# Graph layer and expert layer on one core: the window sums get a full copy, and ten saves of the node rows become one behind the weights

## What is computed

```python
# part 1: graph layer
xs = x[src]
for r in range(4):
    w_r = where(edge_type == r, edge_weight, 0)
    total_msg += (xs @ W_rel[r] + b_rel[r]) * w_r[:, None]
agg = segment_sum(total_msg, dst) / max(segment_sum(edge_weight, dst), 1)
x1 = layer_norm(x + x @ W_self + b_self + agg)
out = layer_norm(x1 + gelu(x1 @ W_ffn1 + b_ffn1) @ W_ffn2 + b_ffn2)
# part 2: 16 experts, the 2 best of each node, on x + out
out = sum_e gate_e * (gelu(xt @ w1e.T + b1e) @ w2e.T + b2e)
```

## Time and profile before

| | |
|---|---|
| median of 3 runs | 654.05 us (651.04 to 654.9) |
| the profiled execution | 651.04 us, of it 649.1 us span |
| PE busy | 528.2 us (81%) |
| DVE busy | 318.7 us (49%) |
| ACT busy | 109.2 us (17%) |
| POOL busy | 228.1 us (35%) |
| chain that ended last | PE 72%, DVE 8%, POOL 7%, DMA 6%, issue 5% |

### The profile page before, as it was taken

One profiled execution on the slowest core, in us unless ns is written; L12 is line 12 of the kernel. 1 busy time (PEld: TensorE's weight loads), 2 busy tenths in 40 slices (PEclk: granted clock), 3 DMA queues, 4 the chain that ended last, 5 costly groups with the idle time before them and its releaser, 6 DMA issues.

```text
span 649.1 us, 7246 instructions
## 1 busy us (share of the span) xinstructions
PE 528.2 (81%) x2292; PEld 355.9 (55%) x2293; DVE 318.7 (49%) x845; ACT 109.2 (17%) x230; POOL 228.1 (35%) x269
## 2 busy tenths in 40 slices
PE   0799999999974999999999999539369879889400
PEld 0588888887722665756657667223046557666200
DVE  5597564321317045986976885857102222222144
ACT  0601011000011322222213212011022222222000
POOL 2750000017777677776773000004700011110173
PEclk9999999989988899999999999855569999999855
DMA  8544342228999676766674492432425477773186
GB/s 291 192 154 149 120 162 97 89 92 259 278 354 354 188 204 199 205 197 182 203 201 126 186 409 87 166 161 114 202 89 176 159 249 264 263 265 113 67 246 223
DMA packets 47682, 125.47 MB, mean 193 GB/s; under 512 B 6480, under 2 KB 7120, under 8 KB 45344
## 3 DMA queue, kind: packets, MB, share of 16 engines
q0 software_dynamic: 17344, 63.20, 31.8%
q1 hardware_dynamic: 27056, 54.95, 22.7%
q10 hardware_dynamic: 3248, 6.89, 3.4%
HBM read 85.70 MB, written 39.32 MB: 193 GB/s over the span
## 4 chain that ended last, share of the span: by engine, by line
PE 72%; DVE 8%; POOL 7%; DMA 6%; issue 5%; ACT 1%; POOLq 0%; SPq 0%; ACTq 0%; DVEq 0%
PE ps L811 11%; PE ps L822 10%; PE ps L751 7%; PE ps L752 7%; PE ps L753 7%; PE ps L944 7%; PE ps L961 6%; PE ps L777 6%; POOL greg L562 3%; DMA greg<-xslot 3%; POOL xslot L536 3%; PE ps L937 2%; PE ps L788 2%; PE ps L843 1%; PE ps L790 1%
## 5 line engine op out<-in xcount | busy, mean ns | idle before, releaser
L515 POOL DMA_INDIRECT greg<-msg,row_i x157 | 153.0, 974 | 156.4 <-DMA msg<-greg 101.6
L751 PE MATMUL ps<-w_hi,xT_hi 128*128 128x512 f32 x200 | 80.0, 400 | 1.7 <-DVE xT_lo L1038 1.7
L752 PE MATMUL ps<-w_lo,xT_hi 128*128 128x512 f32 x200 | 79.5, 398 | 0.0
L753 PE MATMUL ps<-w_hi,xT_lo 128*128 128x512 f32 x200 | 79.3, 397 | 0.0
L811 PE MATMUL ps<-freg,wreg 128*128 128x256 f32 x320 | 72.2, 385 | 0.8 <-ACT freg L610 0.8
L822 PE MATMUL ps<-wreg,freg 128*128 128x512 f32 x160 | 72.1, 598 | 0.0
L811 PEld LDWEIGHTS ps<-freg,wreg 128*128 128x128 f32 x320 | 60.6, 192 | 16.5 <-issue 7.5
L944 PE MATMUL ps<-wreg,freg 128*128 x224 | 56.6, 398 | 0.0
L961 PE MATMUL ps<-wreg,freg 128*128 x112 | 52.7, 593 | 0.9 <-ACT freg L697 0.9
L1342 DVE COPY freg<-ps 128x256 f32<-128x256 f32 x28 | 11.9, 425 | 80.2 <-PE ps L944 80.2
L777 PE MATMUL ps<-greg,sel 128*32 128x512 f32 x320 | 45.6, 629 | 6.8 <-DMA greg<-msg,row_i 6.3
(11 more groups left out here) (169 smaller groups left out, 641.8 us busy)
## 6 DMA issues: line engine op xcount, KB each, us to landing
wreg<-experts POOLq DMA_DIRECT2D x11, 1025.0 KB, 6.8
msg<-greg SPq DMA_DIRECT2D x40, 256.0 KB, 2.0
xslot<-greg SPq DMA_DIRECT2D x1, 8960.0 KB, 25.6
greg<-xslot SPq DMA_DIRECT2D x28, 256.0 KB, 3.8
yslot<-greg SPq DMA_DIRECT2D x28, 256.0 KB, 2.8
wreg<-experts SPq DMA_DIRECT2D x5, 1025.0 KB, 9.4
wreg<-w SPq DMA_DIRECT2D x8, 512.0 KB, 13.6
w_in<-w_rel ACTq DMA_DIRECT2D x3, 1024.0 KB, 6.1
```

Of the source, the lines that this page charges most:

```text
L515: nc.gpsimd.indirect_dma_start(gath[:, c % RING, :], None, msg, bass.IndirectOffsetOnAxis(ap=row_i[:, c:c + 1], axis=0)).then_inc(s_gath[c ...
L751: nc.tensor.matmul(bank(t % 5), xT_hi[:, at], w_hi[:, i, wk], start=(k == 0), stop=False)
L752: nc.tensor.matmul(bank(t % 5), xT_hi[:, at], w_lo[:, i, wk], start=False, stop=False)
L753: mm = nc.tensor.matmul(bank(t % 5), xT_lo[:, at], w_hi[:, i, wk], start=False, stop=(k == KD - 1))
```

## The change

It has two parts. The sums of each step are copied to a new buffer `q_all` in SBUF first, a second pass over the bank makes `q_hi`, and VectorE works out `q_lo` from `q_all`; the next window sums wait for ScalarE's two copies instead of VectorE. And the ten writes of `own_rows` become one write of 2560 KB, issued behind the eight loads of the weights.

```diff
@@ the buffers
+        q_all = sb("q_all", [P, D])
@@ SyncE
-            for t in range(NT):
-                sp.wait_ge(s_evac, FREE + NT * REL + t + 1)
-                sp.dma_start(own_rows[t * P:(t + 1) * P, :], work[:, t, :]).then_inc(s_own, 16)
             sp.wait_ge(s_prod, NT * (REL + 1))
             for k in range(KD):
                 sp.dma_start(w1_v[:, k, :], w1[k * P:(k + 1) * P, :]).then_inc(s_ffw, 16)
             for k in range(0, KF, 2):
                 sp.dma_start(w2_v[:, k:k + 2, :],
                              w2[k * P:(k + 2) * P, :].rearrange("(k p) n -> p k n", p=P)).then_inc(s_ffw, 16)
+            sp.wait_ge(s_evac, FREE + NT * (REL + 1))
+            sp.dma_start(own_rows.rearrange("(t p) d -> p t d", p=P), work[:, :, :]).then_inc(s_own, 16)
+
             sp.wait_ge(s_zeros, 1)
@@ ScalarE
             def sums_out(s):
                 act.wait_ge(s_q, s + 1)
+                after(act, s_qlo, s)
+                nc.scalar.copy(q_all[:, :], bank(B_Q)).then_inc(s_qc, 1)
                 after(act, s_l2, s - 1)
                 nc.scalar.copy(q_hi[:, s % 2, :], bank(B_Q)).then_inc(s_qc, 1)
@@ TensorE
             def window_sums(s):
-                after(pe, s_qlo, s)
+                after(pe, s_qc, 2 * s)
@@ VectorE
             def low_sums(s):
-                dve.wait_ge(s_qc, s + 1)
+                dve.wait_ge(s_qc, 2 * s + 2)
                 after(dve, s_l2, s - 1)
-                v.tensor_tensor(q_lo[:, s % 2, :], bank(B_Q), q_hi[:, s % 2, :], ALU.subtract).then_inc(s_qlo, 1)
+                v.tensor_tensor(q_lo[:, s % 2, :], q_all[:, :], q_hi[:, s % 2, :], ALU.subtract).then_inc(s_qlo, 1)
@@ VectorE, ahead of fast_first_norm(0)
-                    dve.wait_ge(s_own, 16 * NT)
+                    dve.wait_ge(s_own, 16)
```

## The result

The changed kernel takes 676.29 us (median of 4 runs, 674.59 to 677.49) against 654.13 us (4 runs of the kernel before): a ratio of 1.0348, 95% interval 1.0312 to 1.0384, or 22.2 us more. The forecast was 676.5. The profiled execution took 674.45 us, of it 672.5 us span.

What follows compares the result with a forecast made beforehand. Between 184 and 211 us, VectorE's, the weights' and the gathers' strands meet at TensorE, which bounds the chain (72%). Save wait 22.0, clock 0.9 and copy 0.3 make 23.2 us; between two bases, 676.5 us, range 667 to 685.

Steps and rivals of the forecast that it cites:

- The place of the loss and its price: VectorE's norm of tile 0 waits for the save, starting at 216.7 instead of 194.69 us: 22.0 us.
- The rate of the queue: SyncE's queue: weights land at about 204.4 us, then the save at 204 GB/s beside gathers, its last 0.25 MB at 368.
- the 207 GB/s that equal turns were to give: Save beside gathers: equal turns between queues would give it 207 of 414 GB/s, next to the forecast's own 204.
- The strand moves as a piece: From tile 0's norm to tile 1's transposes (194.69 to 210.78 us) no slack; all shifts together, plus 0.9 us for the clock.
- The copy: ScalarE's added copies to `q_all` delay `q_lo` in the pair loop's rounds 1 and 2: 0.3 us, bounds 0 and 1.2.
- the spot that the prediction called tight: End of VectorE's run in the pair loop: `q_lo` ready at 280.22 us, TensorE's add at 280.33, 0.1 us of slack.
- (a): Rival: the save runs almost free of the gathers, landing at 211.5 us, 16.8 late; 669 to 672 us; chance 0.08.
- single-transfer fit: Skill page's formula, 2.0 us plus bytes at 436 GB/s: 8.0 us for the save, landing at 212.4.
- (b): Rival: the second copy is uncovered in all 15 pair-loop steps, 8.9 us on top; 683 to 686 us; chance 0.06.
- (c): Rival: the save lands by 194.69 us, before tile 0's norm, so not slower; 648 to 654 us; chance 0.02.
- (d): Rival: the save overtakes the weights, TensorE's transposes wait for them, about +7 to +8 us; 659 to 662; chance 0.03.
- The base: Starting time for the sum: profiled execution 651.04 us gives 674.2, three-run median 654.05 gives 677.3; forecast set at 676.5.

Runs made afterwards that it cites:

- e5: Kernel before, no `q_all`, the save as one 2560 KB write behind the weights, issued twice, VectorE waiting for both: 680.92 us beside 654.27, ratio 1.0406.
- e6: Kernel before, no `q_all`, the save as one 2560 KB write on ScalarE's queue while SyncE issues the weights: 668.85 us, ratio 1.023.
- e7: Kernel before with only the copy to `q_all`, its ten early saves kept: 652.43 us beside 654.27, ratio 0.9984.
- e4: Kernel before, no `q_all`, the save as one 2560 KB write ahead of the weights, after all ten tiles: 699.75 us, ratio 0.9989, on a slower chip.
- e3: Kernel before, no `q_all`, the ten 256 KB writes kept as ten but moved behind the weights: 711.35 us, ratio 1.0172, on a slower chip.
- control: Kernel before with only one register operation added ahead of each of 39 expert-stage waits: 695.0 us beside 693.56, ratio 1.0064.

## Why the prediction was right

*The place of the loss and its price.* Right. The save landed 37.7 us after the first weight was issued (180.71 to 218.41); the prediction had 37.6 (179.1 to 216.7). What shifted the landing was the products' end, 1.6 us later in this execution. In five kernels whose products are the same it lies between 177.9 and 181.1 on the chips without late sums, so this belongs to the execution, not to the change. Of the 23.7 us by which the norm starts later, 22.1 are left for the change, where 22.0 was forecast.

*The rate of the queue.* Right, but for its end. The last weight landed 25.0 us after the first was issued (it went out at 184.8 and took 20.9 us, to 205.7), where the prediction had 25.3, and the save 12.7 us behind it, where it had 12.3. From 205 to 214 us the two queues moved 209 and 204 GB/s, where it had 210 and 204. The end was wrong: it took the gathers to have landed by 216 and the last 0.25 MB of the save to go alone at 368 GB/s, in 0.7 us. The queues from 214 to 219 us:

```profile
q0 software_dynamic: 400, 1.31, 66.3%
q1 hardware_dynamic: 141, 0.26, 13.5%
```

The gathers' backlog took the engines, and the save's last 0.26 MB lasted until it landed at 218.4. The two misses, 0.3 and 0.4 us, nearly cancel. The rate of a write alone was met only in e5. And the 207 GB/s that equal turns were to give took all packets as equally large: by e6 those of the save hold 2.05 KB and the gathers' 3.28, so equal turns would give the save less than half. It got 204 because the gathers asked for no more than their pitch.

*The strand moves as a piece.* Right: 17.0 us from the norm to the transposes in the changed kernel, and in e5 (224.15 to 241.17) and e6 (211.98 to 229.05) too, for 16.1 before. The 0.9 us of it are the add at the clock's lower level: `add_windows(4)` took 2.26 us from 225.85 for 1.27 before, with a granted clock of 0.50.

*The copy.* 0.3 us was forecast, with bounds of 0 and 1.2; it cost 0.5, in round 1 alone, and at the spot that the prediction called tight. Round 1, from the sums of step 9 to those of step 13, takes 43.49 us before (255.29 to 298.78), 43.98 in the changed kernel (279.22 to 323.20) and 43.99 in e7 (255.01 to 299.00), where the copy stands alone. The changed kernel there, VectorE and then TensorE, for the earlier trace rows:

```profile
303.98 0.71 DVE L1128 TENSOR_TENSOR q_lo<-q_all,q_hi 128x512 fp32r<-128x512 f32 x1
```

```profile
301.06 3.70 PE L825 MATMUL ps<-wreg,freg 128*128 128x512 f32 x8
304.79 0.47 PE L791 MATMUL ps<-q_hi,shift 128*128 128x512 f32 x1
```

`q_lo` is ready at 304.69 and the add starts 0.10 us later. Before it was ready at 280.22 and the add started at 280.33, and the prediction read 0.1 us of slack. There was more. Matmuls overlap, so the start of the add's first row says little; its second row, the one that reads `q_lo`, says what TensorE lost. Before, in round 1, then in round 2, where `q_lo` was ready 0.5 us ahead of the add:

```profile
277.13 3.70 PE L822 MATMUL ps<-wreg,freg 128*128 128x512 f32 x8
280.90 0.39 PE L790 MATMUL ps<-q_lo,shift 128*128 128x512 f32 x1
...
320.60 3.70 PE L822 MATMUL ps<-wreg,freg 128*128 128x512 f32 x8
324.37 0.40 PE L790 MATMUL ps<-q_lo,shift 128*128 128x512 f32 x1
```

In both it starts 3.77 us behind the product's start, so round 1 lost nothing before. In the changed kernel it is 4.04 us (301.06 to 305.10): 0.27 us lost. The next add loses 0.21 in the same way (3.89 for 3.68 us). Counted from the round's start, `q_lo` starts 24.76 us in, for 24.24 before: VectorE's run in the round starts later by most of one copy of 0.59 us, and of the 0.5 us about a half was covered at the first of these adds. In round 2 nothing shows. e5 and e6, which have no copy, take 43.48 us for round 1, as before.

The total of 226.8 us hides this, because the part ahead of round 1 was shorter. Its first stretch, from the sums of step 5 to those of step 6, in the changed kernel, in e7 and in e5:

```profile
236.49:248.21 11.72, 11.72 (x56) 7.66 (x55) 0.96 (x2) 4.83 (x8) 6.03 (x6) 0.85 0.38 101
```

```profile
212.11:223.98 11.87, 11.87 (x55) 7.80 (x54) 0.96 (x2) 4.84 (x8) 8.30 (x10) 0.84 0.66 185
```

```profile
242.22:253.56 11.34, 11.34 (x56) 7.65 (x55) 0.95 (x2) 4.35 (x7) 5.93 (x7) 0.88 0.42 108
```

The same stretch took 12.44 us before with 0.80 granted. In e5, and in e6 with 11.30 us, it is shortest, and neither has the copy: so it isn't the copy that gives this time back, but an earlier return of the clock to full, and what brings that about stays open.

*The rivals.* (a) The save free of the gathers: no, at 204 GB/s it is not; and the single-transfer fit from the Trainium skill that stood beside it (page "DMA: Bandwidth & Descriptors", section "Anatomy of one DMA", a fit of transfers that GpSimd issues: an estimate of 8.0 us) comes near only to e5's second write, which landed 7.2 us behind another one; the save of the changed kernel took 32.6 us, or 12.7 behind the last weight. (b) The copy uncovered in every step: no, 0.5 us in one round and not 8.9. (c) The save in time: no. (d) The save ahead of the weights on its queue: it wasn't; e4 shows that order, at no cost on its chip; for the first chip the estimate there is 2 to 4 us, where the prediction had 7 to 8.

*The base.* The sum against the profiled execution gave 674.2 and the profiled execution of the changed kernel took 674.45. The medians differ by 22.2 us, 1.0 less than the sum; the forecast between the two bases lost that again. That 676.5 and 676.29 lie so near is luck in part: in the traces the products ended 1.6 us later and the experts' part took 1.3 us less, neither was forecast, and they nearly cancel, as do the 0.7 us gained ahead of round 1 and the 0.5 and 0.3 us lost in round 1 and behind round 3.

## What to carry to other kernels

A transfer that nobody waits for can become the one that all wait for when it is moved behind others on its queue. Its landing is worked out from the bytes ahead of it and the rate that is left beside the other queues, and compared with the time at which its waiter arrives; whether it was one write or ten mattered little here, and another queue gave it its turns earlier (14.9 us of wait for 22.0), not a free path.

## What the runs showed of the hardware

- Three busy queues drew the same number of packets in 15 us (814, 812, 816) while they moved 2.67, 1.86 and 1.67 MB. Two queues, one of them the gathers at their pitch, drew 583 and 902 in 9 us, at 414 GB/s in all.
- One queue alone, writing 2560 KB from SBUF to HBM, moved 410 GB/s over 3 us (e5).
- Issuing can block. In e5 SyncE's second write of 2560 KB took 18.15 us to issue, and in e3 the ten writes took up to 5.04 us each, for 0.32 before:

```profile
184.52 0.49 SPq L414 DMA_DIRECT2D own_rows<-work  x1
185.06 18.15 SPq L415 DMA_DIRECT2D own_again<-work  x1
```

- The same kernel took 654, 694 and 702 us on three chips. On the slower two ScalarE started on TensorE's sums 1 to 7 us after their end in 10 to 13 of the 20 steps, and in none of the last three. `control` has it too, so neither the copy nor the save causes it; what does stays open.
